# Relation stage of a graph network kernel: gathered rows as 16-bit planes, turned by transposing transfers

## The reference, cut to what matters

```python
seg = edge_type * n + dst
agg = segment_sum(x[src], seg, num_segments=N_REL * n)
cnt = segment_sum(ones, seg, num_segments=N_REL * n)
mean = agg.reshape(N_REL, n, -1) / maximum(cnt, 1.0).reshape(N_REL, n, 1)
h1 = einsum('rni,rio->no', mean, W_rel) + x @ W_root + b_rgcn   # N_REL = 34, W_rel[r] is 768 x 768
```

## Time and profile before

| what | us |
|---|---|
| median of three runs (3869.45 to 3874.69) | 3874.68 |
| the profiled execution's own time | 3877.03 |
| its span, from the first to the last instruction | 3875.4 |
| PE busy | 3574.6 |
| L1930, the 6840 matmuls of the relation stage, PE busy | 1238.4 |
| ACT busy | 1668.2 |
| POOL busy | 1766.3 |

### The profile page before, as it was taken

The page is one execution under the profiler, slowest core; times in us unless marked ns, Lnnn a source line. Parts: engine busy times, 40 slices in busy tenths (PEclk is TensorE's granted clock), DMA queues, the critical chain, the costliest instruction groups (busy, mean ns, idle before and its releaser), DMA issues.

```text
span 3875.4 us, 56876 instructions
## 1 busy us (share of the span) xinstructions
PE 3574.6 (92%) x18232; PEld 2941.2 (76%) x18233; DVE 1916.4 (49%) x2739; ACT 1668.2 (43%) x2919; POOL 1766.3 (46%) x1330
## 2 busy tenths in 40 slices
PE   8978969999799896599989999999999999989998
PEld 4644549999798896233337999999999999965598
DVE  7426788887434546999854333223332231023334
ACT  1106878888533212599952333333333333300021
POOL 6888888665200000777002444444444444357600
PEclk9988979999999998899999999999999999999999
DMA  3321123333322213211034555555555553379901
GB/s 108 106 46 22 28 58 88 93 79 79 106 90 97 81 49 106 81 41 41 28 106 156 187 181 169 186 187 187 182 168 186 187 187 114 101 263 305 268 17 68
DMA packets 176798, 468.18 MB, mean 121 GB/s; under 512 B 46099, under 2 KB 62538, under 8 KB 176676
## 3 DMA queue, kind: packets, MB, share of 16 engines
q0 software_dynamic: 59584, 185.70, 16.0%
q1 hardware_dynamic: 83972, 190.43, 15.0%
q10 hardware_dynamic: 33120, 90.52, 6.7%
HBM read 346.22 MB, written 119.79 MB: 120 GB/s over the span
## 4 chain that ended last, share of the span: by engine, by line
PE 41%; ACT 7%; POOL 5%; issue 3%; DVE 2%; DMA 1%; SPq 0%; POOLq 0%; DVEq 0%; ACTq 0%
PE ps L1930 31%; POOL work L2011 5%; ACT work L1310 4%; PE ps L1918 3%; ACT ps L1301 3%; PE ps L1593 3%; PE ps L306 2%; PE ps L298 1%; DVE work L1132 1%; PE ps L1247 1%; DVE work L1160 0%; ACT work L1320 0%; DMA ct<-x_d 0%; DMA work<-msg_d,ct 0%; PE ps L324 0%
## 5 line engine op out<-in xcount | busy, mean ns | idle before, releaser
L1930 PE MATMUL ps<-wsplit,xsplit 128*128 x6840 | 1238.4, 338 | 2.7 <-DVEq L1869 2.7
L1930 PEld LDWEIGHTS ps<-wsplit,xsplit 128*128 128x128 f32 x6840 | 1183.0, 188 | 2.9 <-issue 2.9
L1896 POOL TENSOR_TENSOR xsplit<-ct,xsplit 128x768 fp32r<-128x768 f32 x190 | 368.7, 1940 | 298.0 <-ACTq L1962 297.9
L1866 DVE CAST wsplit<-wplain 128x768 fp32r<-128x768 f32 x204 | 117.2, 575 | 761.0 <-PE ps L1930 755.2
L1310 ACT ACTIVATE work<-ps,work 128x418 f32<-128x418 f32 x720 | 438.5, 632 | 107.3 <-PE ps L1220 101.6
L1967 ACT ACTIVATE ct<-ps,invs 128x768 f32<-128x768 f32 x190 | 171.6, 903 | 711.9 <-PE ps L1930 711.9
L1257 PE MATMUL ps<-hbuf,work 128*128 128x193 f32 x2400 | 454.8, 327 | 16.2 <-DVE work L1174 13.1
L1257 PEld LDWEIGHTS ps<-hbuf,work 128*128 128x128 f32 x2400 | 407.1, 190 | 44.0 <-issue 16.7
L1301 ACT ACTIVATE ps<-work,lr 128x418 f32<-128x418 f32 x720 | 431.4, 633 | 6.2 <-DMA work<-lrow_d 6.2
L1160 DVE SCALAR_TENSOR_TENSOR work<-work,cnt 128x1250 f32<-128x1250 f32 x240 | 349.7, 1457 | 133.8 <-ACT work L1310 131.5
L1891 POOL DMA_INDIRECT ct<-x_d,relrec x190 | 200.4, 1055 | 456.8 <-PE ps L1918 445.2
(11 more groups left out here) (217 smaller groups left out, 4253.7 us busy)
## 6 DMA issues: line engine op xcount, KB each, us to landing
wplain<-in_L_gnn_W_rel SPq DMA_DIRECT2D x34, 2304.0 KB, 9.7
msg_d<-ct ACTq DMA_DIRECT2D x190, 384.0 KB, 2.6
work<-lrow_d SPq DMA_DIRECT2D x47, 625.0 KB, 3.9
feat_d<-work ACTq DMA_DIRECT2D x30, 386.0 KB, 2.6
hbuf<-feat_d SPq DMA_DIRECT2D x60, 193.0 KB, 2.5
gat_d<-work POOLq DMA_DIRECT2D x12, 960.0 KB, 5.4
xplain<-gat_d SPq DMA_DIRECT2D x30, 384.0 KB, 3.2
wplain<-x_d SPq DMA_DIRECT2D x20, 384.0 KB, 3.1
```

Source lines behind the costliest of these rows:

```text
L1896: g.tensor_tensor(xlo7[:, k % XW, :], xt7[:, k % 2].rearrange("p c n -> p (c n)"), xhi7[:, k % XW, :].bitcast(F32), ALU.subtract).then_inc ...
L1930: last = pe.matmul(ps[:, 4 + 2 * (u % 2) + h, 0:HALF], x[:, u, c * P:(c + 1) * P], w[:, bass.ds(base + (c * D + h * HALF), HALF)], start=( ...
```

## The change

After the change x3 is also stored in a second form, `x3p_d`: each row of 768 float32 is written as 768 low half words followed by 768 high half words (16 bits each, 3072 bytes as before). In the root stage ACT makes these planes with one copy of 128x1536 half words per tile, and SP stores them. In the relation stage POOL gathers rows of `x3p_d` in place of `x3_d`, into GW = 2 slots and three tiles ahead. The turning is no longer done by PE: ACT issues a transposing DMA from `rows7` to one of two slots `plane7`, which turns the twelve 128x128 blocks of half words of a tile. ACT then joins the two planes back to float32 with one copy of 128x1536 half words into `xt7`, waits for it, and makes `xhi7` with a second copy, now from `xt7`. In ACT's queue the order is: store of tile k, take of tile k + 3, turn of tile k + 5. The turn waits for the gather of k + 5 to land, and only behind this wait is `s_take7` raised, for which POOL's `low(k + 3)` waits. POOL's gather of a tile waits until the transposing DMA of the tile two before it has landed.

```diff
@@ root stage, act_root
             for j in range(NT):
+                act.wait_ge(s_ready6, j + 1)
+                if j >= 2:
+                    act.wait_ge(s_turn7[j % 2], 16 * (j // 2))
+                act.activation(plane7[:, j % 2, :].rearrange("p (t n) -> p t n", t=2),
+                               z6[:, j, :].bitcast(U16).rearrange("p (n t) -> p t n", t=2), ACT.Copy).then_inc(s_plane6, 1)
                 W_ROOT.take(act, j // 2, j % 2)
@@ relation stage, buffers
-        GW = XW = 4
+        GW, XW = 2, 4
-        rows7 = c7(GW * D).rearrange("p (u r n) -> p u r n", u=GW, r=1)
+        rows7 = c7(GW * 2 * D, U16).rearrange("p (u n) -> p u n", u=GW)
+        plane7 = c7(2 * 2 * D, U16).rearrange("p (u n) -> p u n", u=2)
@@ sp_rel
+            def planes(j):
+                sp.wait_ge(s_plane6, j + 1)
+                sp.dma_start(x3p_d[j * P:(j + 1) * P, :], plane7[:, j % 2, :]).then_inc(s_turn7[j % 2], 16)
             for j in range(2, NT):
                 sp_parts(sp, j)
+                planes(j - 2)
+            for j in range(NT - 2, NT):
+                planes(j)
@@ pool_rel
                 if k >= GW:
-                    g.wait_ge(s_turn7, k - GW + 1)
+                    g.wait_ge(s_turn7[k % GW], TURN0 + 16 * (k // GW))
-            for k in range(GW):
+            for k in range(AHEAD7):      # AHEAD7 = 3
                 gather(k)
@@ pe_rel: turn() and its calls are gone
-                for c in range(KC):
-                    last = pe.transpose(ps[:, 2 * (u % 2) + c // 3, (c % 3) * P:(c % 3 + 1) * P], rows7[:, u % GW, 0, c * P:(c + 1) * P], ident[:, :])
-                last.then_inc(s_turn7, 1)
@@ act_rel
+            def turn(u, gathers, taken=True):
+                act.wait_ge(s_gath[u % GW], 16 * gathers)
+                if taken:
+                    act.sem_inc(s_take7, 1)
+                act.dma_start_transpose(plane7[:, u % 2, :].rearrange("p (c r) -> p c r", r=P), rows7[:, u % GW, :]).then_inc(s_turn7[u % 2], 16)
-                step.count(act.activation(xt7[:, u % 2].rearrange("p (a b) n -> p a (b n)", a=2),
-                                          ps[:, 2 * (u % 2):2 * (u % 2) + 2, 0:HALF], ACT.Copy))
-                step(act.activation(halves(xhi7[:, u % XW, :]), ps[:, 2 * (u % 2):2 * (u % 2) + 2, 0:HALF], ACT.Copy))
-                act.sem_inc(s_take7, 1)
+                x = xt7[:, u % 2].rearrange("p c n -> p (c n)")
+                step(act.activation(x.bitcast(U16).rearrange("p (n t) -> p t n", t=2),
+                                    plane7[:, u % 2, :].rearrange("p (t n) -> p t n", t=2), ACT.Copy))
+                step(act.activation(xhi7[:, u % XW, :], x, ACT.Copy))
                 for u in range(XW):
                     k = XW * i + u + 2
                     store(k, u + 2, 2 * i + 1 + (u + 2) // 2)
-                    take(k + 3, u + 5)
+                    take(k + 3, u + 5, 2 * i + (u + 5) // 2 + 1)
+                    turn(u + 7, 2 * i + (u + 7) // 2 + 1)
```

More of the change, by code:

```diff
@@ L94, in build @@
         x3_d = dram("x3_d", (NP, D))
+        x3p_d = dram("x3p_d", (NP, 2 * D), U16)
         msg_d = dram("msg_d", (RT * P, D))
@@ L1779, in build @@
         s_st6 = two("x3_stored")
-        s_ready6, s_bias6 = sem("x3_ready"), sem("root_bias_in")
+        s_ready6, s_bias6, s_plane6 = sem("x3_ready"), sem("root_bias_in"), sem("x3_planes_ready")
         brow6 = work[:, 3 * KC * D:3 * KC * D + D]
@@ L1802, in product @@
                         v.wait_ge(s_st6[u], 16 * (NT // 2))
+                        v.wait_ge(s_turn7[u], TURN0)
                 if j >= 7:
@@ L1829, in pool_root @@
                 g.wait_ge(s_st6[u], 16 * (NT // 2))
+                g.wait_ge(s_turn7[u], TURN0)
         whi7, wlo7 = wsplit[:, 0:2 * KC * D], wsplit[:, 2 * KC * D:4 * KC * D]
-        GW = XW = 4
+        GW, XW = 2, 4
         c7 = Carve(ct[:, :].bitcast(F32), NT * CW // 2)
-        rows7 = c7(GW * D).rearrange("p (u r n) -> p u r n", u=GW, r=1)
+        rows7 = c7(GW * 2 * D, U16).rearrange("p (u n) -> p u n", u=GW)
+        plane7 = c7(2 * 2 * D, U16).rearrange("p (u n) -> p u n", u=2)
         xt7 = c7(2 * D).rearrange("p (u c n) -> p u c n", u=2, c=KC)
@@ L1843, in build @@
         s_gath = [sem(f"rows_gathered{u}") for u in range(GW)]
-        s_turn7, s_take7, s_prod7, s_emp7, s_lo7 = (sem(n) for n in ("turned7", "taken7", "product7", "emptied7", "low_parts7"))
+        s_turn7 = two("plane_slot_moved7_")
+        TURN0 = 16 * (NT // 2)
+        s_take7, s_prod7, s_emp7, s_lo7 = (sem(n) for n in ("taken7", "product7", "emptied7", "low_parts7"))
         s_split7 = sem("weights_split7")
@@ L1885, in dve_rel @@
             relation(R - 1, 1)
+        AHEAD7 = 3
         def pool_rel(g, step):
@@ L1889, in gather @@
                 if k >= GW:
-                    g.wait_ge(s_turn7, k - GW + 1)
-                g.indirect_dma_start(out=rows7[:, k % GW, 0, :], out_offset=None, in_=x3_d,
+                    g.wait_ge(s_turn7[k % GW], TURN0 + 16 * (k // GW))
+                g.indirect_dma_start(out=rows7[:, k % GW, :], out_offset=None, in_=x3p_d,
                                      in_offset=bass.IndirectOffsetOnAxis(relrec[:, 2 * k:2 * k + 1], 0)).then_inc(s_gath[k % GW], 16)
@@ L1902, in pool_rel @@
             for k in range(RT):
-                if k + GW < RT:
-                    gather(k + GW)
+                if k + AHEAD7 < RT:
+                    gather(k + AHEAD7)
                 low(k)
@@ L1933, in messages @@
                 last.then_inc(s_prod7, 1)
-            for k in range(2):
-                turn(k, 1, k)
             pe.wait_ge(W_ROOT.emptied, W_ROOT.b["emptied"] + NT + 2)
-            whole = (RT - 2) // GW
+            whole = RT // XW
             with pe.Fori(0, whole) as i:
[L1940 to L1947, removed]
+                for u in range(XW):
+                    messages(XW * i + u, u)
+            for k in range(whole * XW, RT):
+                messages(k, k % XW)
         def act_rel(act, step):
@@ L1951, in act_rel, with take @@
             act.wait_ge(W_ROOT.product, W_ROOT.all_products)
-            def take(k, u):
-                act.wait_ge(s_turn7, k + 1)
+            def turn(u, gathers, taken=True):
[3 more added lines that the diff above has]
+                act.dma_start_transpose(plane7[:, u % 2, :].rearrange("p (c r) -> p c r", r=P), rows7[:, u % GW, :]).then_inc(s_turn7[u % 2], 16)
+            def take(k, u, turns):
+                act.wait_ge(s_turn7[u % 2], TURN0 + 16 * turns)
                 if not isinstance(k, int) or k >= 2:
@@ L1975, in act_rel @@
             for k in range(2):
-                take(k, k)
-            take(2, 2)
+                turn(k, 1, taken=False)
+            for k in range(3):
+                take(k, k, k // 2 + 1)
+                turn(k + 2, k // 2 + 2)
             for k in range(2):
                 store(k, k, 1)
-                take(k + 3, k + 3)
-            whole = (RT - 5) // XW
+                take(k + 3, k + 3, (k + 3) // 2 + 1)
+                turn(k + 5, (k + 5) // 2 + 1)
+            whole = (RT - 7) // XW
             with step.loop(whole, 3 * XW) as i:
@@ L1989, in act_rel @@
                 if k + 3 < RT:
-                    take(k + 3, k + 3)
+                    take(k + 3, k + 3, (k + 3) // 2 + 1)
+                if k + 5 < RT:
+                    turn(k + 5, (k + 5) // 2 + 1)
+                elif k + 3 < RT:
+                    act.sem_inc(s_take7, 1)
             for u in range(2):
```

## The result

The changed kernel takes 3934.01 us (median of 4 runs, 3925.53 to 3953.5) against 3872.06 of the kernel before (4 runs). The ratio is 1.0172, with a 95% interval of 1.0136 to 1.0208. The forecast was 3756, faster by 3%; the time lies in the stated range, but on the other side of no change. The profiled execution took 3929.81 us, its span is 3928.2.

What follows compares the result with a forecast made beforehand. PE, 92% busy and never idle in the relation stage's loop, was taken as the bound. -124.6 (transposes) + 5 (start) + 1 (root stage) = -118.6 us gave 3758.4, 3756 against the median; stated range 3738 to 3980.

Steps and rivals of the forecast that it cites:

- PE's part: Relation stage: without 1140 transposes PE takes 6.25 us a tile, 1190.6 us in place of 1315.2, 124.6 less.
- ACT, per tile: ACT's queue in the relation stage: 4.4 us a tile plus the transposing issue, within PE's 6.25 us.
- x: Time ACT's queue is held by issuing one transposing transfer: 0.34 us taken, PE-bound up to 1.85.
- The term beside it: ACT's other work per relation-stage tile: 4.4 us, with 1.43 for the copy of 1536 half words.
- the first rival: ACT's queue bounds the relation stage, issue 1.85 to 2.5 us, still faster: 3803 us at 2.1; chance 0.09.
- ACT's queue held: Relation stage: ACT's queue is held for the whole transfer, 2.6 us, 7.0 us a tile, 3898 us; chance 0.12.
- The figure of 32 cycles a tile: The page's figure for a transposing transfer, said to lead to the queue-held case: 2.6 us, 3898 us; chance 0.12.
- The DMA engines: Relation stage: the new transfer adds 1.2 to 2.3 us a tile; engines 78 to 96% busy, under the limit.
- Weights: Relation-stage loads, once in 5.6 tiles: slower loading is hidden by DVE's waits, costing only if 20 us slower.
- The loop of slots: Row slots of the relation stage: a transfer lands in about 3 to 5 us, where 7.5 is allowed.
- Start: Start of the relation stage: first messages 4.3 to 6.7 us later, taken as 5.
- Root stage: Ten added ACT copies of 1.43 us and ten SP stores, mostly covered: 1 us put down.

Runs made afterwards that it cites:

- e10: Changed kernel with the transposing transfers issued by SP, not ACT, and the weight loads of relations 1 to 33 left out: 3742 us, 0.968 of the kernel before.
- e13: Changed kernel with the rounded copy on POOL and transposing transfers of only six of twelve blocks: 3762 us, 0.972 of the kernel before.
- e1: Changed kernel with the join of the planes over only half of each tile's columns (768 of 1536 half words): 3859 us, 0.998 of the kernel before.
- e2: Changed kernel with transposing transfers of only six of the twelve blocks (low half words): 3811 us, 0.987 of the kernel before.
- e3: Changed kernel without the loads of the weights of relations 1 to 33: 3816 us, 0.988 of the kernel before.
- e7: Changed kernel with each 2304 KB load of weights cut in three pieces issued over three tiles: 3865 us, 0.998 of the kernel before.
- e11: Changed kernel with the rounded copy given to POOL, loads in one piece: 3847 us, 0.994 of the kernel before.
- e9: Changed kernel with the weight loads in three pieces and the rounded copy given to POOL, message stores kept in ACT's queue: 3889 us, 1.006 of the kernel before.

## Why the prediction was wrong, point by point

- *PE's part was right.* Without transposes a tile takes PE 6.25 us, and e10 and e13 ran at it, though both leave work out. The 124.6 us were there to be had.
- *ACT, per tile: the step that failed.* "I take the low end, since the issue is the row of the same engine and size" took x as 0.34 us. It is 1.29 at the least, 1.52 in the median and 2.2 in the mean. The issue of a store in rows of 3072 bytes did not price that of a transfer in 1536 pieces. The term beside it, 4.4 us, was 5.1: the join took 1.96 us and not 1.43. I had scaled a copy out of PSUM of whole words (0.80 ns an element) to a strided copy of half words in SBUF; e1 gives (1.96 - 1.08) / 768 = 1.15 ns. Together 7.3 us against 4.7. The 2.2 us lie in the range of the first rival (1.85 to 2.5), which was still to be faster; with 5.1 beside them they are slower. The case that I gave 0.12 and put at 3898, ACT's queue held, was the nearest in time, though the queue is held for the issue and not until the landing (4.4 us).
- *The figure of 32 cycles a tile.* The Trainium skill, "DMA: Bandwidth & Descriptors", has it in the table of its section "Why a DMA increments its semaphore by 16 and not by 1", and it led to an estimate of 2.6 us for the issue. The mean of 2.2 lies near it, but not for its reason: the undisturbed issue is 1.5, and e2 shows that 48 tiles less take off 0.28 us in the median, 6 ns each, where the estimate has 27 (2.6 us / 96). The measurement decides.
- *The DMA engines.* The line through two packet sizes gave 24 ns for 256 bytes and 2.34 us a tile. In e10 SP's queue holds nothing else, and its row reads

```profile
q1 hardware_dynamic: 150528, 37.76, 34.7%
```

  0.347 x 16 x 600 / 150528 = 22 ns, and 2.2 us for each of 96 tiles. The size was right. The reading was not: "under the limit, though not far" treated the share as a mean that either fits or doesn't. In the changed kernel, at 82%, the issues stretch while a load of weights runs, and without the loads (e3) they don't. The 261 GB/s of the Trainium skill, "DMA: Bandwidth & Descriptors" (latency and other measured facts), gave 1.5 us; here a turn of 393 KB costs 2.2 us of all engines, 181 GB/s.
- *Weights.* I wrote that a slower load is hidden. The load is; what it does to the transposing issue in ACT's queue is not. e3 and e7 price that at 118 and 69 us.
- *The loop of slots.* The landing was 4.4 us in the median, in my 3 to 5, but up to 17.2. In the changed kernel this loop hardly counts (2 of 82 turns waited); it is what bounds as soon as ACT's queue is relieved and the bursts of loads stay (e1, e11), or the engines are at 93% (e9).
- *Start.* 7.6 us later against 5. The first two issues took 1.7 each. `s_take7` waited for a gather as reckoned, but from the gather's issue to the turn behind it 7.1 us passed (2088.18 to 2095.27) and not 4.8; a load of weights was issued beside it. *Root stage*: no cost, as good as the 1 us put down.

## What to carry to other kernels

Before work is moved from a full engine to the DMA path, price the issue too: it occupies the queue of the engine that issues it, in front of that engine's next work, and here it stretched beside a large load. Add the engine's own queue up per tile as if it were the bound. When a shared resource goes from half to four fifths busy, look at the largest burst beside it and not at the mean; spreading that burst was worth nearly as much here (69 us) as taking a copy off the bound engine (87 us), and the two together were worse than either, since a loop of two slots stood behind them. And a change that overloads its new place may pay when half of the work is moved.

## What the runs showed of the hardware that I had not expected

- The issue of a transposing transfer of 128 x 1536 half words holds ACT's queue for 1.29 us at the least, of six blocks for 1.23; a plain store of the same 384 KB takes 0.34. Beside loads of 2304 KB it took up to 8.87 us in the changed kernel, without them up to 2.28 (e3).
- It moves in packets of 256 bytes (under 512 B: 130836 packets for 82 tiles), 22 ns each in e10.
- A copy that joins two planes of half words costs ACT 1.15 ns an element, against 0.80 for float32 out of PSUM.
- PE's granted clock fell to 0.95 in a stretch where it was idle for 10%, and was 1.00 in e7 where it was idle for 34 of 600 us in waits of at most 2 us; in the loop of the changed kernel waits of up to 10.9 us occur.
